# An attention kernel on one core: score products in groups of 3, 3 and 2 per two key tiles, values two key tiles late, and half of the running maxima read bank by bank

## The reference

```python
q, k, v = x @ Wq + bq, x @ Wk + bk, x @ Wv + bv      # 16 heads of 16 channels
q, k = rotary(q), rotary(k)
probs = softmax(q @ k.T / sqrt(16))                  # 2048 x 2048 for each of 32 heads
x = layernorm(x + probs @ v)
r = sigmoid(mix_r(x) @ W_r.T)                        # mix: with the token before
out = layernorm(x + r * (square(relu(mix_k(x) @ W_k.T)) @ W_v.T))
```

## Time and profile before

| | us |
|---|---|
| median of 3 runs (lowest, highest) | 1455.68 (1455.48, 1456.43) |
| the profiled execution: device time, span | 1454.18, 1452.1 |
| busy in the span: PE, DVE, ACT, POOL | 1432.9, 1375.0, 1188.2, 305.6 |
| clock granted to TensorE, mean | 1.000 (the 2.4 GHz level) |

### The profile page before, as it was taken

One profiled execution on the slowest core, in us unless ns is written; L12 is line 12 of the kernel. 1 busy time (PEld: TensorE's weight loads), 2 busy tenths in 40 slices (PEclk: granted clock), 3 DMA queues, 4 the chain that ended last, 5 costly groups with the idle time before them and its releaser, 6 DMA issues.

```text
span 1452.1 us, 31356 instructions
## 1 busy us (share of the span) xinstructions
PE 1432.9 (99%) x12952; PEld 600.0 (41%) x12952; DVE 1375.0 (95%) x1459; ACT 1188.2 (82%) x2153; POOL 305.6 (21%) x277
## 2 busy tenths in 40 slices
PE   8999999999999999999999999999999999999998
PEld 6663333333333333333333333333333333333575
DVE  5779999999999999999999999999999999999496
ACT  4448888888888888888888888888888888888745
POOL 3441221032103210032103210231102000001174
PEclk9999999999999999999999999999999999999999
DMA  7755112232223211222223222311122323200242
GB/s 229 239 145 166 26 31 38 36 95 38 37 37 96 38 30 23 80 39 37 37 38 96 37 37 38 92 25 26 30 37 37 51 38 52 46 2 5 44 115 102
DMA packets 73184, 88.79 MB, mean 61 GB/s; under 512 B 48786, under 2 KB 58642, under 8 KB 66786
## 3 DMA queue, kind: packets, MB, share of 16 engines
q1 hardware_dynamic: 72482, 86.00, 28.1%
q10 hardware_dynamic: 560, 0.79, 0.2%
HBM read 29.51 MB, written 14.16 MB: 30 GB/s over the span
## 4 chain that ended last, share of the span: by engine, by line
PE 96%; ACT 1%; DVE 1%; DMA 1%; issue 0%; POOL 0%; POOLq 0%; ACTq 0%; DVEq 0%
PE pv_ps L692 39%; PE scores L778 31%; PE ring_ps L673 14%; PE scores L630 2%; PE ring_ps L720 2%; PE scores L855 2%; ACT probs L957 1%; PE pv_ps L702 1%; PE scores L646 1%; PE pv_ps L630 1%; PE scores L839 1%; PE pv_ps L839 1%; DMA rope<-tables 1%; PE ring_ps L744 0%; PE pv_ps L646 0%; PE scores L744 0%
## 5 line engine op out<-in xcount | busy, mean ns | idle before, releaser
L1302 DVE TENSOR_REDUCE tile_max<-ring_ps 128x1 f32<-128x1024 f32 x1024 | 1232.4, 1217 | 31.3 <-PE ring_ps L673 22.9
L957 ACT ACTIVATE probs<-scores 128x512 f32<-128x512 f32 x1984 | 1073.0, 595 | 158.9 <-PE scores L778 119.6
L778 PE MATMUL scores<-q_stack,k_stack 50*128 50x512 f32 x1984 | 731.4, 448 | 6.9 <-ACT probs L957 6.7
L673 PE MATMUL ring_ps<-k_stack,q_stack 48*128 48x512 f32 x2048 | 733.5, 443 | 0.0
L692 PE MATMUL pv_ps<-probs,v_aug 128*32 128x256 f32 x7936 | 628.7, 391 | 0.0
L778 PEld LDWEIGHTS scores<-q_stack,k_stack 50*128 50x128 f32 x1984 | 294.9, 185 | 415.6 <-ACT probs L957 399.1
L692 PEld LDWEIGHTS pv_ps<-probs,v_aug 128*32 128x32 f32 x7936 | 160.6, 108 | 355.8 <-issue 179.2
L673 PEld LDWEIGHTS ring_ps<-k_stack,q_stack 48*128 48x128 f32 x2048 | 300.0, 184 | 6.9 <-DVE tile_max L1302 3.3
L1062 POOL TENSOR_TENSOR neg_cuts<-neg_max,zeros 128x16 fp32r<-128x16 f32 x31 | 6.8, 219 | 492.8 <-DVE neg_max L1275 492.8
L1054 POOL TENSOR_TENSOR v_aug<-v_all,b_v_s 128x256 f32<-128x256 f32 x32 | 23.5, 736 | 310.4 <-PE pv_ps L692 252.9
L1071 POOL TENSOR_TENSOR ctx_part<-ctx_turn,recip 128x256 f32<-128x256 f32 x32 | 20.0, 625 | 259.2 <-DVE recip L1329 259.2
(11 more groups left out here) (146 smaller groups left out, 619.6 us busy)
## 6 DMA issues: line engine op xcount, KB each, us to landing
k_stack<-rope SPq DMA_DIRECT2D x61, 256.0 KB, 5.2
q_stack<-rope SPq DMA_DIRECT2D x32, 256.0 KB, 4.4
k_stack<-rope SPq DMA_DIRECT2D x63, 128.0 KB, 4.8
qk_raw<-probs SPq DMA_DIRECT2D x28, 256.0 KB, 3.9
rope<-qk_raw SPq DMA_DIRECT2D x7, 1024.0 KB, 4.8
rope<-qk_raw SPq DMA_DIRECT2D x14, 512.0 KB, 6.5
q_stack<-rope SPq DMA_DIRECT2D x34, 128.0 KB, 4.9
z_s<-x_tok SPq DMA_DIRECT2D x2, 2048.0 KB, 12.7
```

What stands on the lines that cost most here:

```text
L673: mm = pe.matmul(ring_ps[k % 2][:, c * TOK:(c + 1) * TOK], q_stack[rows, slot, qt * P:(qt + 1) * P], k_stack[rows, slot, lo + c * TOK:lo + ...
L778: mm = pe.matmul(score_ps[n % SCORE_BANKS][:, :], k_stack[rows, slot, kt * P:(kt + 1) * P], queries[:, j], start=True, stop=True)
L957: act.activation(probs[:, kt % 2, j, :], score_ps[n % SCORE_BANKS][:, :], ACT.Exp, scale=SCALE).then_inc(exps_done, 1)
L1302: dve.reduce_max(tile_max[:, h % 2, unit // 2, unit % 2:unit % 2 + 1], slot[:, :], AX.X)\
```

## The change

- The values of a key tile are multiplied two key tiles later, not one (`PV_LAG`), and `probs` has three buffers. Over two key tiles, 8 pairs, TensorE now does three pairs, the whole values of one key tile, three pairs, the first half of the next key tile's values, two pairs, and its second half (`VALUES`, `values_after`). Before, it was two pairs and a half, four times.
- The ring is counted in banks: TensorE waits for the one bank that it writes, and signals each one. Of the two units of a key tile, VectorE reduces the first as before, in one instruction, and the second in two, one per bank (`max` with an odd unit, and `rest`). `tile_max` has three columns for each query tile.
- The turn of a head before comes one key tile later, and in the last period the values of two key tiles of the head before are done in whole form, and the wait for the turn comes after the next score products.
- In the opening, the pieces of values stand between the four blocks of the first quad, each held in a bank of the ring, and 18 pieces, not 16, come before the first unit. To make room, some small buffers share the place of weights that are done with.

```diff
@@ -47,8 +47,12 @@
 STAGES = 8
 UNITS = TILES * BLOCKS
 SCORE_BANKS = 3
-PV_CREDIT = 2
-RING_CREDIT = 2
+PROB_BUFS = 3
+PV_CREDIT = PROB_BUFS
+PV_LAG = 2
+VALUES = {2: (0, 1), 5: (0,), 7: (1,)}
+RING_CREDIT = 4
+MAX_PARTS = 3
 MAX_UNITS = 2 * TILES
 LEAD = 4
 EARLY = 2 * LEAD
@@ -89,29 +93,31 @@
 
 WORK = list(projections())
 EARLY_V = BLOCKS + TILES // 2
-BEFORE_MAXIMA = EARLY_V + 4
+BEFORE_MAXIMA = EARLY_V + 6
 LAST_IN_BANK = [max(range(n, len(WORK) - 1, SCORE_BANKS + 1)) for n in range(SCORE_BANKS)]
 WARM_UP = 10
-FIRST_ORDER = [0, BLOCKS, BLOCKS + 1, 1, BLOCKS + 2, 2, 3, BLOCKS + 3]
+FIRST_ORDER = [i for n in range(BLOCKS) for i in (n, BLOCKS + 2 * n, BLOCKS + 2 * n + 1)]
 BLOCK_DONE = {n: max(i for i, (_, a, t) in enumerate(WORK) if (a, t) == (QUADS // BATCH - 1, n)) for n in range(BLOCKS)}
 PLACE = {n: place for place, n in enumerate([*FIRST_ORDER, *range(len(FIRST_ORDER), len(WORK))])}
 STORED = {(g, n): s for s, (g, n) in enumerate((g, n) for kind, g, n in WORK if kind == "qk" and g > 0)}
 
 
+def maxima(h, unit):
+
+    return [("max", h, unit), ("max", h, unit + 1), ("rest", h, unit + 1)]
+
+
 def period_ops(h):
 
     for kt in range(TILES):
         ops = []
-        for u in (2 * kt + EARLY, 2 * kt + EARLY + 1):
-            if u < MAX_UNITS:
-                if h + 1 <= LAST:
-                    ops.append(("max", h + 1, u))
-                    if u == MAX_UNITS - 1:
-                        ops.append(("cut", h + 1, 0))
-            elif h + 2 <= LAST:
-                ops.append(("max", h + 2, u - MAX_UNITS))
-        if 0 < h < LAST and kt == 0:
-            ops.insert(1, ("turn", h - 1, 0))
+        owner, u = (h + 1, 2 * kt + EARLY) if kt < TILES - LEAD else (h + 2, 2 * kt + EARLY - MAX_UNITS)
+        if owner <= LAST:
+            ops += maxima(owner, u)
+            if u + 2 == MAX_UNITS:
+                ops.append(("cut", owner, 0))
+        if 0 < h < LAST and kt == 1:
+            ops.insert(2, ("turn", h - 1, 0))
         if 0 < h < LAST and kt == RECIP_CYCLE:
             ops.append(("recip", h - 1, 0))
         if kt == STAT_CYCLE and 0 <= h - STAT_HEAD < POOL_BLOCKS * TPB:
...
@@ -606,10 +621,10 @@
 
                 kind, a, i = WORK[n]
                 bank = banks[n]
-                if n >= 3 * BLOCKS:
+                if EARLY_V <= n < EARLY_V + BLOCKS:
+                    pe.wait_ge(quad0_taken, n - EARLY_V + 1)
+                elif n >= 2 * BLOCKS:
                     pe.wait_ge(evacuated, n - 2 * BLOCKS + 1)
-                elif n >= 2 * BLOCKS:
-                    pe.wait_ge(quad0_taken, n - 2 * BLOCKS + 1)
                 if kind == "qk":
                     block = a * BATCH // QUADS * BLOCKS + i
                     m = a % (QUADS // BATCH) * P
...
@@ -653,7 +668,6 @@
 
             def maximum(k, h, unit):
 
-                pe.wait_ge(ring_freed, k + 1)
                 buf, qt, lo = h % STACKS, unit // 2, unit % 2 * 2 * TOK
                 copy = h >= FIRST_COPY and unit < EARLY
                 place = h + 1 if copy else h
...
@@ -670,10 +684,10 @@
                 for c in range(2):
                     if c and first <= unit < last:
                         rows, slot = stack_rows(twin, 0, ROWS), slot_of(twin)
+                    pe.wait_ge(ring_freed, 2 * k + c + 1)
                     mm = pe.matmul(ring_ps[k % 2][:, c * TOK:(c + 1) * TOK], q_stack[rows, slot, qt * P:(qt + 1) * P],
                                    k_stack[rows, slot, lo + c * TOK:lo + (c + 1) * TOK], start=True, stop=True)
-                    if c:
-                        mm.then_inc(ring_filled, 1)
+                    mm.then_inc(ring_filled, 1)
                     yield
 
             def ring_ops(ops, k):
...
@@ -686,11 +700,10 @@
             def pv_half(h, kt, half):
 
                 t = slice(half * (TOK // 2), (half + 1) * (TOK // 2))
+                pe.wait_ge(exps_done, SCORE_BANKS + item(h, kt, BLOCKS - 1) + 1)
                 for j in range(BLOCKS):
-                    if half == 0:
-                        pe.wait_ge(exps_done, SCORE_BANKS + item(h, kt, j) + 1)
                     mm = pe.matmul(pv_ps[j * VCOLS:(j + 1) * VCOLS, t], v_aug[:, h % 2, kt, :],
-                                   probs[:, kt % 2, j, t], start=kt == 0 and half == 0, stop=kt == TILES - 1,
+                                   probs[:, (h * TILES + kt) % PROB_BUFS, j, t], start=False, stop=kt == TILES - 1,
                                    skip_group_check=True)
                 if half == 1:
                     mm.then_inc(pv_done, 1)
@@ -698,16 +711,32 @@
             def pv_whole(h, kt):
 
                 for j in range(BLOCKS):
-                    pe.wait_ge(exps_done, SCORE_BANKS + item(h, kt, j // WIDE * WIDE) + WIDE)
-                    mm = pe.matmul(pv_ps[j * VCOLS:(j + 1) * VCOLS, :], v_aug[:, h % 2, kt, :], probs[:, kt % 2, j, :],
-                                   start=kt == 0, stop=kt == TILES - 1, skip_group_check=True)
+                    if j % 2 == 0:
+                        pe.wait_ge(exps_done, SCORE_BANKS + item(h, kt, j + 1) + 1)
+                    mm = pe.matmul(pv_ps[j * VCOLS:(j + 1) * VCOLS, :], v_aug[:, h % 2, kt, :],
+                                   probs[:, (h * TILES + kt) % PROB_BUFS, j, :], start=kt == 0, stop=kt == TILES - 1,
+                                   skip_group_check=True)
                 mm.then_inc(pv_done, 1)
 
-            def pv(h, kt):
-
-                for half in range(2):
-                    pv_half(h, kt, half)
-
+            def values_after(h, kt, j):
+
+                halves = VALUES.get(kt % 2 * BLOCKS + j, ())
+                tile = h * TILES + kt - PV_LAG
+                if tile < 0:
+                    if (kt, len(halves)) == (0, 2):
+                        project(len(WORK) - 1)
+                    return
+                owner, t = divmod(tile, TILES)
+                if len(halves) == 2:
+                    if t == 0:
+                        if owner == 0:
+                            pe.wait_ge(evacuated, len(WORK) - BLOCKS)
+                        pe.wait_ge(v_aug_ready, owner + 1)
+                        after(pe, pv_turned, owner)
+                    pv_whole(owner, t)
+                else:
+                    for half in halves:
+                        pv_half(owner, t, half)
 
             def project_r(n, width):
...
@@ -746,10 +775,12 @@
                                            start=True, stop=True)
                         mm.then_inc(scores_ready, WIDE)
                     if kt == 0:
-                        pv(LAST - 1, TILES - 1)
-                        pe.wait_ge(v_aug_ready, LAST + 1)
-                        pe.wait_ge(pv_turned, LAST)
+                        for tile in range(TILES - PV_LAG, TILES):
+                            pv_whole(LAST - 1, tile)
                     else:
+                        if kt == 1:
+                            pe.wait_ge(v_aug_ready, LAST + 1)
+                            pe.wait_ge(pv_turned, LAST)
                         pv_whole(LAST, kt - 1)
                 pe.wait_ge(exps_done, SCORE_BANKS + item(LAST, TILES - 1, 0))
                 for _ in range(R_FILL):
...
@@ -924,20 +939,24 @@
             act.wait_ge(w_v_in, DMA)
             act.activation(w_v_high, w_v_s, ACT.Copy).then_inc(w_v_split, 1)
             split_high(1)
+            take(BLOCKS)
             split_high(2)
+            take(BLOCKS + 1)
             split_high(3)
-            take(BLOCKS)
             cut_high(0)
-            take(BLOCKS + 1)
+            take(BLOCKS + 2)
+            take(BLOCKS + 3)
             cut_high(1)
             act.wait_ge(w_qk_in, DMA)
             act.activation(w_qk_high[:, :, P:], w_qk_s[:, :, P:], ACT.Copy).then_inc(w_qk_split, 1)
-            take(BLOCKS + 2)
+            take(BLOCKS + 4)
+            take(BLOCKS + 5)
             cut_high(2)
-            take(BLOCKS + 3)
+            take(BLOCKS + 6)
+            take(BLOCKS + 7)
             cut_high(3)
             act.wait_ge(b_first_in, DMA)
-            for n in range(BLOCKS + 4, len(WORK) - 1):
+            for n in range(EARLY_V, len(WORK) - 1):
                 take(n)
                 for block, last in BLOCK_DONE.items():
                     if n == last:
...
@@ -1271,7 +1291,7 @@
 
                 for kind, h, unit in ops:
                     if kind == "cut":
-                        dve.wait_ge(ring_freed, RING_CREDIT + k)
+                        dve.wait_ge(ring_freed, RING_CREDIT + 2 * k)
                         dve.tensor_reduce(neg_max[:, :], tile_max[:, h % 2], AX.X, ALU.max, negate=True)\
                             .then_inc(neg_ready, 1)
                         if h == LAST:
...
@@ -1293,14 +1313,18 @@
                             dve.wait_ge(y_pool_ready, h // TPB + 1)
                             dve.wait_ge(quad_ready, QUADS - 1)
                         flip(h // TPB, h % TPB)
-                    else:
-                        slot = ring_ps[k % 2]
```

(35 more changed lines are left out.)

43 lines of the change are left out of this document (14 added, 29 removed).

## The result

| | before | after |
|---|---|---|
| median us (lowest to highest, runs) | 1455.58 (1453.03 to 1456.43, 4) | 1409.73 (1409.08 to 1411.55, 4) |
| profiled execution us, span | 1454.18, 1452.1 | 1411.55, 1409.8 |

The ratio is 0.9691, with an interval of 0.9677 to 0.9706: 45.9 us less, where 32.6 were forecast. In the traces, the first head's score products begin at 98.58 before and at 96.32 after, the last period at 1332.1 and 1289.7, and its rest takes 120 us in both. So 2.3 us come from the opening, 40.1 from the 31 heads and nothing from the end. Of the other 3.5, 3.2 are the distance of the two profiled executions from their medians (1454.18 to 1455.58, 1411.55 to 1409.73), and 0.3 lies outside the spans.

The account below looks back on a forecast made before the run. TensorE was taken as the bound, VectorE 2.5 us per head behind and the bound after the change. Heads -36.6, statistics and transposes +6.4, opening -2.4 sum to -32.6: 1423 us against 1455.68, with 1403 to 1448 for 8 in 10.

Parts of the forecast that it names:

- TensorE was the bound, with VectorE close behind: Heads before the change: TensorE sets the pace at 39.76 us a head, VectorE only 2.5 us per head behind.
- TensorE's round would be 4.63: TensorE's work over two key tiles in the heads: 4.63 us with the new groups, 4.96 before.
- The row of the third pair: One place of a head with four pairs in a row: the third pair comes 0.24 after the second.
- VectorE becomes the bound, with units at 1.13 and banks at 0.60: VectorE's reductions in the heads: 4.66 us a round, more than TensorE's 4.63.
- The price cited from the Trainium skill: VectorE reductions: 1.0417 ns a column and about 75 ns per instruction, a round of 4.72, result about 1433.
- The other rule cited from the Trainium skill: VectorE: next operation starts only when the pipe is empty; taken at its word, the case of 1538 us.
- the 0.02 a round that I added for late banks: Ring in the heads: an allowance for banks that come late, raising VectorE's round to 4.68.
- the small operations: VectorE's turn, cut, transpose of the negatives and reciprocals: 1.14 us in a head, hidden before, now paid.
- the band of 1413 to 1438: Kernel time if VectorE sets the pace with a bank at 0.585 to 0.615; given 60%.
- Statistics and transposes, 6.4: VectorE work in some heads, hidden before by TensorE's pace: 6.4 us set against the gain.
- The opening, 2.4: Opening: TensorE's wait of 2.41 for the low part of the fourth block goes, winning 2.4 us.
- The rival that was to make it slower: VectorE's single-bank reductions cost more; at 0.66 a bank the kernel takes 1478 us; chance 13%.

Follow-up runs that it names:

- pairs_of_two: Changed kernel with TensorE back to two pairs and a half of values, four times in two key tiles; banks, lag and third buffer kept: 1454.51 us.
- short_reads: Changed kernel with each single-bank reduction reading 256 of its 512 columns, so part of the maxima is left out: 1370.9 us.
- two_halves: Changed kernel with the whole values issued as two halves of 256 queries, one behind the other: 1410.55 us.
- all_bank: Changed kernel with the even units too read bank by bank, in two reductions of 512 columns: 1441.4 us.
- power_on_gpsimd: Changed kernel with the reciprocal of the sums made on GpSimd as a power of -1 instead of on VectorE: 1408.64 us.
- old_opening: Changed kernel with the opening's order, banks and counts as in the kernel before: 1414.62 us.
- all_whole: Changed kernel with every unit of the maxima read whole, in one reduction: 1624.35 us.
- lag_one: Changed kernel with values one key tile late instead of two and the turn one key tile earlier, three buffers kept: 1443.96 us.

## Why the prediction was right

- **TensorE was the bound, with VectorE close behind.** Right: with the groups taken back and all else kept, the time is that of the kernel before (pairs_of_two), and before the change TensorE never waited for a ring buffer between 300 and 1300 us.
- **TensorE's round would be 4.63.** Right to the hundredth, where VectorE lets it (short_reads). The row of the third pair, read in the one odd place of a head, held for the steady state. One reading in the sum was wrong without harm to it: the 0.14 that it won on the values was put down to the whole form, 1.00 against 2 x 0.57, but two halves in a row take 1.00 too (two_halves), and did so in the trace of before.
- **VectorE becomes the bound, with units at 1.13 and banks at 0.60.** Right: 1.131 and 0.598 in the trace, 4.65 a round; adding reductions costs what they take (all_bank), relieving VectorE wins until TensorE's own round is reached (short_reads), and VectorE's reductions wait 0.2 us in all between 130 and 1290 us. The price cited from the Trainium skill ("Vector Engine (DVE) Microarchitecture Reference", section "Measured stream behaviour on trn2"), about 75 ns beside the columns, would have given 0.61 and 1.14; the runs show some 65 ns. The 1.14 that the prediction read in the trace of before and found to agree is two rounded starts: unrounded it is 1.131. The other rule cited from the Trainium skill ("VectorE: DVE Perf Modes", section "The DRAIN you can't avoid"), that the next operation does not start until the pipe is empty, does not hold for these reductions: a bank lasts 0.67 and is followed after 0.60. The same section says that an operation that is not held starts earlier, which the prediction left out.
- **The size was off by 13.3 us.** The term is the head: 38.58 forecast, 38.25 measured, 0.33 x 31 = 10.2. Of the 0.33, 0.16 are the 0.02 a round that I added for late banks and that did not come, since TensorE's 4.63 leaves it 0.02 a round to make up a late product; 0.05 is rounding (8 x 4.654 for 8 x 4.66); and 0.12 is the small operations, priced at 1.14 by the distance to the next start, while they cost 1.03, because what follows the reciprocal, the turn or the transposed negatives is shorter by 0.05, 0.02 and 0.03. The first head won less than a regular one by this trace (40.42 to 39.61), with a spell of lower clock in it (last section); in two_halves and power_on_gpsimd, which have none there, it takes 38.1. The other 3.5 us are for the most part the distance of the profiled executions from their medians; in the changed kernel's the two spells cost some 2.5 us (an estimate: 1.5 in the first head and 1 in the opening, against the traces without them). The time lies 3 us outside the band of 1413 to 1438 that the prediction gave its own case, though this is that case: the band let only the bank's price vary.
- **Statistics and transposes, 6.4, no longer hidden.** Right: seven heads take 38.65, four 38.9 to 39.3 and two 38.4 and 38.5, which is 6.2 over 38.25 in all.
- **The opening, 2.4.** 2.3 by the two traces, but that is luck: the changed kernel's opening has a spell of lower clock and that of before has none. Like with like the new order is worth more, 2.6 to 3.7 without a spell and 4.3 with one (old_opening).
- **The rival that was to make it slower** needed banks at 0.64; they are at 0.60. What the prediction did not price is how close the kernel stands to another fall: with its banks read whole it loses 215 us.

## What to carry over

When two engines are nearly equal, sum up both for the new round and take the larger; then check the loop that goes through the shared buffers, product by product, since a reader that frees two banks at once can cost more than any engine's sum shows (all_whole). When work is grouped in another way, ask what the change between two kinds of work costs: here it was all that was won, and a row with two pieces of one kind side by side, present in the trace of before, would have told its price. What an instruction costs is the distance to the next start, but for a small operation also look at what its successor takes: part of the price comes back there. A row from an odd place of a trace (a third pair, a late reduction) can price a state that the kernel does not yet have.

## What the runs showed of the hardware

In the changed kernel's opening TensorE has no idle time between 10 and 96 us, and its granted clock dips, which the trace of before does not show there. Two stretches of the changed kernel (us, busy by engine, granted clock, DMA share, GB/s):

```profile
0.00:10.00 10.00, 6.64 (x47) 2.82 (x47) 4.50 (x8) 3.37 (x5) 7.99 (x11) 1.00 0.71 246
10.00:30.00 20.00, 20.00 (x127) 18.70 (x128) 17.63 (x23) 11.63 (x17) 7.11 (x5) 0.91 0.72 245
```

0.91 over 20 us is a spell of some 3.4 us at the 1.2 GHz level (10.15 to 13.56); there is a second one in the first head (from 102.31). What TensorE did before the clock fell differs. The openings of the changed kernel, all_bank, all_whole, two_halves and lag_one (there twice as long) have a spell that begins between 9.6 and 12.1 us, and that of old_opening has one at 22.5. In all six TensorE waited 2.0 to 3.2 us just then: the wait ended at most 1.3 us before the spell began, or at most 0.7 after. But a wait of 2.0 in power_on_gpsimd and one of 2.4 in the kernel before brought none. The spell near 102 us, which all_whole and short_reads have as well (from 104.25 and 100.44), stands in a stretch where TensorE's longest wait was 0.4 us. The openings with the new order end at 94.0 to 95.9 us in the six traces without an early spell, at 96.3 to 96.8 in the four with one, and at 97.83 with the double one. What sets a spell off was not tried.
